# Attention on one core: when o is split, when V's remainder is taken, and where the widest exponential stands on ScalarE

## The chip, the cores and the metric

The kernel runs on one core of a Trainium2 chip. A core has TensorE (PE, matrix products; its loads of weights are PEld), VectorE (DVE), ScalarE (ACT), GpSimd (POOL) and SyncE (SP, which starts transfers). Each works through its own program in order, and they meet only at semaphores. The metric is the device time of one execution in microseconds, the median of several runs. Lower is better.

## What is computed

The reference, cut to what matters:

```python
xn = layernorm(x)                                   # x: 2 x 1024 x 256, float32
q = (xn @ Wq + bq).reshape(b, 16, t, 128)           # 16 heads, 128 columns each
k = (xn @ Wk + bk).reshape(b, t, 16, 128).transpose(0, 2, 3, 1)
v = (xn @ Wv + bv).reshape(b, t, 16, 128).transpose(0, 2, 1, 3)
weights = softmax(q @ k / sqrt(128) + causal_mask)
o = (weights @ v).transpose(0, 2, 1, 3).reshape(b, t, 2048)
result = x + (o @ Wo + bo) + ffn(xn)                # ffn: gate, up and down, weights of 4 bits
```

The change touches only the attention part.

## The kernel before

**Split products.** Every operand of a product is kept as a rounded part (`_hi`) and a remainder (`_lo`, what the rounding left out), and every product is three matmuls: hi by hi, hi by lo, lo by hi (`split_matmul`, L41 to L45). So each result in PSUM is emptied twice: ACT writes the rounded part, then DVE subtracts it from the same bank and writes the remainder. Only after both is the bank free.

**Heads and steps.** 32 heads (2 batches of 16) are worked one after the other, each in 8 steps, one for each tile of 128 query rows. Tile i needs the keys of tiles 0 to i, so its scores are (i + 1) x 128 wide; tile 7 is the widest, 1024. PE's step `i` is: the transposes of the tile three steps back (`LAG` = 3), the job that `FIRST_AT` names, the scores, the job that `EARLY_AT` names, on odd steps a product of weights with V (`with_v`), and the job that `LATE_AT` names. `with_v` in step 5 and step 7 makes quarters 0 and 1 of the head's o, in step 1 and step 3 of the next head quarters 2 and 3. Two quarters are one half of o, a full bank `O`.

**Jobs.** K0 and K1 are the two halves of the next head's K, Va and Vb parts of V, O0a to O1b products of the two halves of the last head's o with Wo. All of them use the one bank `M` (PSUM bank 5): `run` makes each wait until the one before is emptied (`job_lo_done`). Their places are K0 in step 0, K1 in 1, O0a in 2, O0b and Va in 3, O1a in 5, O1b in 6 and Vb in 7.

**A tile's way.** PE writes the scores; DVE copies them to `probs` with the mask and takes the maximum (L962); ACT takes the exponential and the row sum (`exps`, L763); POOL takes the reciprocal (L845) and scales the row (L848); three steps later PE transposes the row into one of two banks `T`, in pieces of at most 512 columns; ACT writes `pt_hi` (L749), DVE `pt_lo` (L916). A piece's transposes wait until `pt_lo` of the piece two before is written, since they reuse its bank.

**The order on ACT and DVE** is written out by hand, step by step. On ACT a step is: Va's rounding of the step before, `pt_high` of the tile three back, the `FIRST_AT` job, `o_high` (L756, in steps 0 and 4: half 0 and half 1 of the last head's o), the exponential of the tile before if that tile isn't in `EAGER`, the `EARLY_AT` job, and for tiles in `EAGER` (1, 3 and 7) their own exponential at the end. DVE has the same frame with `pt_low` (L916), `o_low` (L921), Va's remainder (L876, in step 4), the maximum (L962) and the emptying of jobs (`k_lo` L871, `acc` L883).

In heads 7, 15 and 23 the queries of the next eight heads are prepared between the steps (`q_step`, `q_ahead`, with `wq_hi` L732, `wq_lo` L889, `q_all` L904); these are called Q heads below. `q_low` and the remainders of the weights of V, K and Wo run on POOL as well.

Of the kernel before, what the change touches and what calls it, by code (L numbers as in the profile page):

```python
# [36 lines left out]
def flat(ap):  # L37
    return ap.rearrange("p a b -> p (a b)")
# [495 lines left out]
def attention(nc, sh, d, out):  # L534

    NH = BATCH * HEADS
    GROUP = N // (SEQ // HEADS)
    GROUPS = NH // GROUP
    TILES = SEQ // P
# [11 lines left out]
    with ExitStack() as c:  # L551
# [39 lines left out]
        EARLY_AT = {1: "K1", 3: "O0b", 5: "O1a"}  # L591
        LATE_AT = {3: "Va"}
        AT = [FIRST_AT[0], EARLY_AT[1], FIRST_AT[2], EARLY_AT[3], LATE_AT[3], EARLY_AT[5], FIRST_AT[6], FIRST_AT[7]]
        EAGER = (1, 3, 7)
        Q_AFTER = {2: (0,), 3: (1,), 4: (2, 3), 5: (4, 5), 6: (6, 7)}
        START = {0: ("K", 0, 1), 2: ("V", 0, 0), 4: ("V", 0, 1)}

# [22 lines left out]
        q_steps = lambda h, i: Q_AFTER.get(i, ()) if new_group(h) else ()  # L620
        eager = lambda h, i: i in EAGER or len(q_steps(h, i)) > 1

# [14 lines left out]
        def v_view(tile, pair, j):  # L637
            return tile[:, v_slots(pair), 2 * j:2 * j + 2, :]
# [55 lines left out]
        @block.scalar  # L694
        def _(act):
            def wo_high(h):
                act.wait_ge(wo_loaded, 16 * (h + 1))
                nc.scalar.activation(wo_hi[:, h % 2, :], wo_in[:], ACT.Copy).then_inc(wo_hi_done, 1)

            def vw_high(pair):  # L700
                act.wait_ge(vw_loaded, 32 * (pair + 1))
                if pair:
                    act.wait_ge(job_done, nth[("V", pair - 1, 3)])
                nc.scalar.activation(flat(vw_hi[:]), flat(vw_in[:]), ACT.Copy).then_inc(vw_hi_done, 1)

            def kw_high(pair):
                act.wait_ge(job_done, nth[("K", 2 * pair - 1, 1)])
                kv_high(nc, act, sh, 16 * (pair + 1))

            def evacuate(job):  # L710

                if job is None or job[0] == "O":
                    return
                act.wait_ge(job_done, nth[job])
                if job[0] == "K":
                    _, h, half = job
                    ins = nc.scalar.activation(k_hi[:, h % 2, half * N:(half + 1) * N], M, ACT.Identity,
                                               bias=bk[:, h % HEADS:h % HEADS + 1])
                else:
                    ins = nc.scalar.activation(v_view(v_hi, *job[1:]), M_V, ACT.Copy)  # L720
                ins.then_inc(job_hi_done, 1)

            def q_split(h, half):

                rows = q_all[:, h % GROUP, half * 32:half * 32 + 32, :].rearrange("p r c -> p (r c)")
                nc.scalar.activation(q_hi[:, half, :], rows, ACT.Copy).then_inc(q_hi_done, 1)  # L726

            def wq_high(n):

                act.wait_ge(wq_loaded[n % LOADS], 16 * (n // LOADS + 1))  # L730
                wait(act, qp_done, n - LOADS + 1)
                nc.scalar.activation(flat(wq_hi[:, n % LOADS, :, :]), flat(wq_in[:, n % LOADS, :, :]), ACT.Copy  # L732
                                     ).then_inc(wq_hi_done, 1)

            def q_ahead(o, u):

                for n in (2 * u + 2, 2 * u + 3):
                    if n < HEADS:
                        wq_high(o * HEADS + n)

            def pt_high(s):

                i = s % TILES
                for ch in range(banks_of(i)):
                    at = chunk_no(s, ch)
                    blocks = min(QT, i + 1 - ch * QT)
                    act.wait_ge(pt_done, at + 1)
                    first = pt_block(i // 2) + ch * QT
                    nc.scalar.activation(  # L749
                        pt_hi[:, first:first + blocks, i % 2 * P:(i % 2 + 1) * P],  # L750
                        T[at % 2][:, 0:blocks * P].rearrange("p (a b) -> p a b", b=P), ACT.Copy
                    ).then_inc(pt_hi_done, 1)

            def o_high(h, half):
                act.wait_ge(pv_done, 4 * h + 2 * half + 2)
                nc.scalar.activation(o_hi[:], O, ACT.Identity, bias=bv[:, h % HEADS:h % HEADS + 1]  # L756
                                     ).then_inc(o_hi_done, 1)

            def exps(s):

                act.wait_ge(max_done, s + 1)
                width = (s % TILES + 1) * P
                nc.scalar.activation(probs[:, s % 4, 0:width], probs[:, s % 4, 0:width], ACT.Exp,  # L763
                                     bias=neg_max[:, s % 16:s % 16 + 1], scale=-1.0,
                                     accum_out=row_sum[:, s % 16:s % 16 + 1]).then_inc(exp_done, 1)

            act.wait_ge(sh["bias_in"], 48)
            wq_high(0)
            wq_high(1)
            evacuate(("K", 0, 0))  # L770
            for u in range(8):
                q_ahead(0, u)
                if u == 1:
                    vw_high(0)
                evacuate(START.get(u))
            act.wait_ge(q_done, HEADS)
            q_split(0, 0)

            for s in range(NH * TILES):
                h, i = divmod(s, TILES)  # L780
                evacuate(job_of(h, LATE_AT.get(i - 1)))
                if s >= LAG:
                    pt_high(s - LAG)
                evacuate(job_of(h, FIRST_AT.get(i)))
                if i in (0, 4) and h > 0:
                    o_high(h - 1, i // 4)
                if i > 0 and not eager(h, i - 1):
                    exps(s - 1)
                evacuate(job_of(h, EARLY_AT.get(i)))
                if i == 1:  # L790
                    act.wait_ge(scores_done, s)
                    q_split(h, 1)
                    if new_group(h):
                        wq_high((h + 1) // GROUP * HEADS)
                        wq_high((h + 1) // GROUP * HEADS + 1)
                    if h % 2 == 1 and (h + 1) // 2 < NH // 2:
                        vw_high((h + 1) // 2)
                if i == 2:
                    wo_high(h)
                if i == 5 and not new_group(h) and h + 1 < NH:  # L800

                    act.wait_ge(scores_done, s)
                    q_split(h + 1, 0)
                if i == 6 and h % 2 == 0 and h // 2 + 1 < NH // 2:
                    kw_high(h // 2 + 1)
                if i == 7 and new_group(h):

                    act.wait_ge(q_done, (h + 1) // GROUP * HEADS + HEADS)
                    q_split(h + 1, 0)
                if eager(h, i):  # L810
                    exps(s)
                for u in q_steps(h, i):
                    q_ahead(h // GROUP + 1, u)

            pt_high(NH * TILES - 3)
            o_high(NH - 1, 0)
            pt_high(NH * TILES - 2)
            pt_high(NH * TILES - 1)
            o_high(NH - 1, 1)
# [42 lines left out]
        def _(dve):  # L862
# [56 lines left out]
            def o_low(h, half):  # L919
                dve.wait_ge(o_hi_done, 2 * h + half + 1)  # L920
                nc.vector.scalar_tensor_tensor(o_lo[:], O, bv[:, h % HEADS:h % HEADS + 1],  # L921
                                               o_hi[:].bitcast(F32), ALU.add, ALU.subtract).then_inc(o_lo_done, 1)
# [17 lines left out]
            for s in range(NH * TILES):  # L940
                h, i = divmod(s, TILES)
                between = FIRST_AT.get(i) == "O0a"
                if s >= LAG:
                    pt_low(s - LAG, 0)
                    if between:
                        evacuate(job_of(h, FIRST_AT[i]))
                    if banks_of((s - LAG) % TILES) > 1:
                        pt_low(s - LAG, 1)
                if not between or s < LAG:
                    evacuate(job_of(h, FIRST_AT.get(i)))  # L950
                if i in (0, 4) and h > 0:
                    o_low(h - 1, i // 4)
                if i - 1 in LATE_AT:
                    evacuate(job_of(h, LATE_AT[i - 1]))
                hurry = EARLY_AT.get(i) == "O1a"
                if hurry:
                    evacuate(job_of(h, EARLY_AT[i]))
# [6 lines left out]
                    -1.0, -MASKED, ALU.add, ALU.min, neg_max[:, s % 16:s % 16 + 1]).then_inc(max_done, 1)  # L964
                if not hurry:
                    evacuate(job_of(h, EARLY_AT.get(i)))
                if i == 1 and new_group(h):
                    wq_low((h + 1) // GROUP * HEADS)
                    wq_low((h + 1) // GROUP * HEADS + 1)
# [6 lines left out]

            end = NH * TILES
            pt_lows(end - 3)
            o_low(NH - 1, 0)
            add_residual(0)  # L980
            add_residual(1)
            evacuate(("O", NH - 1, 0, 0))
# [216 lines left out]
```

## Time and profile before

| | us |
|---|---|
| median of 3 runs | 1319.09 (1319.01 to 1320.17) |
| profiled execution, its own time | 1319.28 |
| its span | 1317.0 |

| engine | busy us | share of the span |
|---|---|---|
| PE | 1232.1 | 94% |
| PEld | 1072.9 | 81% |
| DVE | 947.8 | 72% |
| POOL | 795.8 | 60% |
| ACT | 766.3 | 58% |

The granted clock of TensorE was 0.996 of full speed over the span. The attention part runs from about 330 us to the end. A head without preparation of queries takes 26.7 us.

How to read rows of a timeline: start in us from the span's start, length in us, engine, line, operation, what is written and what is read, the shape, how many of them are merged in the row, and in brackets how long the engine sat idle before it and what released it. A row of a matmul is longer than the distance to the next one, because matmuls are pipelined.

### The profile page before, as it was taken

The page shows a single profiled execution, that of the slowest core. Times are in us where ns is not written, and L with a number is a line of the kernel's source. Part 1 is how long each engine was busy: PE and PEld are TensorE (multiplying, and loading weights), DVE is VectorE, ACT ScalarE, POOL GpSimd, SP SyncE. Part 2 cuts the span into 40 slices and gives each one's busy share as a digit, 9 for nine tenths or more (in the row PEclk, how much of TensorE's full clock was granted, in tenths as well). Part 3 has the DMA queues.
Part 4 walks back from the last instruction along what each step waited for, and adds up shares of the span by engine and source line. Part 5 has one row for each costly group of instructions (what it writes and reads, how often), then busy time and mean ns, then how long its engine had stood idle before and what let it go on. Part 6 is the DMA issues. An engine that isn't in the chain of part 4 may idle for free.

```text
span 1317.0 us, 20858 instructions
## 1 busy us (share of the span) xinstructions
PE 1232.1 (94%) x7468; PEld 1072.9 (81%) x7468; DVE 947.8 (72%) x1734; ACT 766.3 (58%) x1575; POOL 795.8 (60%) x799
## 2 busy tenths in 40 slices
PE   3799999999899999999999999999999999999997
PEld 2677777777678888888888988898888878889886
DVE  7778877888676667676766677767666776667666
ACT  3565555555446656644666665466665636566653
POOL 5566666666447667644766655366766526666662
PEclk9899999999999999999999999999999999999999
DMA  4000000010210000020000001100000110000012
GB/s 94 12 13 13 13 6 12 12 28 5 57 36 21 15 15 22 13 60 22 21 13 13 25 5 53 33 25 5 21 13 14 40 33 13 13 25 5 13 50 83
DMA packets 60986, 32.43 MB, mean 25 GB/s; under 512 B 17120, under 2 KB 60896, under 8 KB 60896
## 3 DMA queue, kind: packets, MB, share of 16 engines
q1 hardware_dynamic: 59280, 29.99, 8.1%
q10 hardware_dynamic: 1616, 1.25, 0.3%
q8 instruction: 56, 0.92, 0.3%
q14 instruction: 34, 0.28, 0.1%
HBM read 29.12 MB, written 2.10 MB: 24 GB/s over the span
## 4 chain that ended last, share of the span: by engine, by line
PE 52%; DVE 11%; ACT 8%; issue 1%; POOL 1%; DMA 0%; DVEq 0%; SPq 0%; ACTq 0%
PE ps L43 15%; PE ps L45 15%; PE ps L44 15%; PE ps L1079 7%; DVE probs L962 3%; ACT probs L763 3%; DVE pt_lo L916 2%; ACT pt_hi L749 2%; DVE o_lo L921 2%; DVE v_lo L876 1%; DVE q_all L904 1%; ACT o_hi L756 1%; ACT v_hi L720 1%; DVE wq_lo L889 1%; DVE acc L883 0%
## 5 line engine op out<-in xcount | busy, mean ns | idle before, releaser
L916 DVE TENSOR_TENSOR pt_lo<-ps,pt_hi 128x512 fp32r<-128x512 f32 (+3 forms) x384 | 204.4, 553 | 217.9 <-ACT pt_hi L749 215.1
L845 POOL TENSOR_TENSOR inv_sum<-row_sum,minus_one 128x1 f32<-128x1 f32 x256 | 141.5, 553 | 295.8 <-ACT probs L763 295.8
L848 POOL TENSOR_TENSOR probs<-probs,inv_sum 128x128 f32<-128x128 f32 (+7 forms) x256 | 296.4, 1158 | 20.1
L763 ACT ACTIVATE probs<-probs,neg_max 128x128 f32<-128x128 f32 (+7 forms) x256 | 198.5, 775 | 144.3 <-DVE neg_max L962 141.6
L749 ACT ACTIVATE pt_hi<-ps 128x512 fp32r<-128x512 f32 (+3 forms) x384 | 173.8, 488 | 93.3 <-PE ps L1079 90.4
L962 DVE CUSTOM_DVE_ANT_0 probs<-ps,mask_row 128x128 f32<-128x128 f32 (+7 forms) x256 | 192.1, 751 | 3.4 <-PE ps L45 0.7
L1079 PE MATMUL ps<-ident,probs 128*128 128x128 f32 x1152 | 172.3, 277 | 9.1 <-DVE pt_lo L916 8.4
L44 PE MATMUL ps<-pt_lo,v_hi 128*128 128x256 f32 (+1 forms) x640 | 177.5, 277 | 0.0
L45 PE MATMUL ps<-pt_hi,v_lo 128*128 128x256 f32 (+1 forms) x640 | 177.2, 277 | 0.0
L43 PE MATMUL ps<-pt_hi,v_hi 128*128 128x256 f32 (+1 forms) x640 | 170.7, 267 | 0.7 <-DVE pt_lo L916 0.7
L269 POOL TENSOR_TENSOR hid_lo<-hid,hid_hi 128x512 fp32r<-128x512 f32 x64 | 83.1, 1298 | 104.8 <-ACT hid_hi L328 104.8
L1079 PEld LDWEIGHTS ps<-ident,probs 128*128 128x128 f32 x1152 | 127.2, 140 | 20.1 <-issue 11.8
L43 PE MATMUL ps<-k_hi,q_hi 128*128 128x512 f32 (+3 forms) x384 | 140.2, 365 | 1.9 <-DVE k_lo L871 1.9
L45 PE MATMUL ps<-k_hi,q_lo 128*128 128x512 f32 (+3 forms) x384 | 133.0, 346 | 0.0
L44 PE MATMUL ps<-k_lo,q_hi 128*128 128x512 f32 (+3 forms) x384 | 132.9, 346 | 0.0
L43 PE MATMUL ps<-xn_hi,w_hi 128*128 128x512 f32 x256 | 106.2, 415 | 22.5 <-DVE hid L448 17.7
L43 PEld LDWEIGHTS ps<-pt_hi,v_hi 128*128 128x128 f32 x640 | 120.2, 188 | 6.2 <-DVE pt_lo L916 0.9
L44 PEld LDWEIGHTS ps<-pt_lo,v_hi 128*128 128x128 f32 x640 | 120.4, 188 | 5.6
L45 PEld LDWEIGHTS ps<-pt_hi,v_lo 128*128 128x128 f32 x640 | 120.6, 188 | 0.0
L825 POOL TENSOR_TENSOR q_lo<-q_all,q_hi 128x512 fp32r<-128x512 f32 x64 | 82.3, 1286 | 51.4 <-ACT q_hi L726 51.4
L45 PE MATMUL ps<-xn_hi,w_lo 128*128 128x512 f32 x256 | 103.0, 402 | 0.0
L44 PE MATMUL ps<-xn_lo,w_hi 128*128 128x512 f32 x256 | 102.8, 401 | 0.0
(109 smaller groups left out, 3006.1 us busy)
## 6 DMA issues: line engine op xcount, KB each, us to landing
wq_in<-in_wq SPq DMA_DIRECT2D x64, 128.0 KB, 2.3
kv_in<-in_wk SPq DMA_DIRECT2D x16, 256.0 KB, 2.7
kv_in<-in_wv SPq DMA_DIRECT2D x32, 128.0 KB, 2.3
wo_in<-in_wo SPq DMA_DIRECT2D x32, 128.0 KB, 2.0
q_all<-in_x SPq DMA_DIRECT2D x1, 2048.0 KB, 9.5
out<-q_all SPq DMA_DIRECT2D x8, 256.0 KB, 2.2
raw<-in_gate SPq DMA_DIRECT2D x18, 64.0 KB, 1.8
raw<-in_up SPq DMA_DIRECT2D x18, 64.0 KB, 2.0
```

What stands on the lines that cost most here:

```text
L43: nc.tensor.matmul(out, w_hi, m_hi, start=start, stop=False)
L44: nc.tensor.matmul(out, w_hi, m_lo, start=False, stop=False)
L45: return nc.tensor.matmul(out, w_lo, m_hi, start=False, stop=stop)
L269: nc.gpsimd.tensor_tensor(hid_lo[:, kk % 4, :], hid[:, kk % 4, :], hid_hi[:, kk % 4, :].bitcast(F32), ALU.subtract).then_inc(hid_lo_done, 1)
L749: nc.scalar.activation(pt_hi[:, first:first + blocks, i % 2 * P:(i % 2 + 1) * P], T[at % 2][:, 0:blocks * P].rearrange("p (a b) -> p a b", ...
L763: nc.scalar.activation(probs[:, s % 4, 0:width], probs[:, s % 4, 0:width], ACT.Exp, bias=neg_max[:, s % 16:s % 16 + 1], scale=-1.0, accum_ ...
L825: nc.gpsimd.tensor_tensor(dst, src, high.bitcast(F32), ALU.subtract).then_inc(done, 1)
L845: nc.gpsimd.tensor_tensor(inv_sum[:, at], row_sum[:, at], minus_one[:], ALU.pow).then_inc(inv_done, 1)
L848: nc.gpsimd.tensor_tensor(row, row, inv_sum[:, at].to_broadcast([P, (i + 1) * P]), ALU.mult).then_inc(probs_done, 1)
L916: nc.vector.tensor_tensor(pt_lo[where], T[at % 2][:, 0:blocks * P].rearrange("p (a b) -> p a b", b=P), pt_hi[where].bitcast(F32), ALU.subt ...
L962: nc.vector.tensor_tensor_reduce(probs[:, s % 4, 0:width], flat(S[place[("S", h, i)] % 2])[:, 0:width], mask_row[:, SEQ - width:SEQ], -1.0 ...
L1079: last = nc.tensor.transpose(T[at % 2][:, n * P:(n + 1) * P], probs[:, s % 4, b * P:(b + 1) * P], ident[:])
```

## The change

It moves instructions and removes none. On ACT and DVE, the split of half 1 of o (`o_high`, `o_low`) goes from step 4 to the end of step 3, and that of half 0 from step 0 of the next head to the end of step 7. Va's remainder on DVE goes from behind `pt_low` and `o_low` to the front of step 4. Tile 7 is no longer in `EAGER`: its exponential goes from the end of step 7 to step 0 of the next head, behind `pt_high` of tile 5 and K0's rounding. The last head's has a place of its own behind the loop. PE's, POOL's and SP's programs are the same.

```diff
-        EAGER = (1, 3, 7)
+        EAGER = (1, 3)
...
                 evacuate(job_of(h, FIRST_AT.get(i)))
-                if i in (0, 4) and h > 0:
-                    o_high(h - 1, i // 4)
-                if i > 0 and not eager(h, i - 1):
+                if i > 0 and not eager(h, i - 1) or i == 0 and h > 0:
                     exps(s - 1)
...
                 if eager(h, i):
                     exps(s)
+                if i == 3 and h > 0:
+                    o_high(h - 1, 1)
+                if i == 7:
+                    o_high(h, 0)
                 for u in q_steps(h, i):
                     q_ahead(h // GROUP + 1, u)
 
+            exps(NH * TILES - 1)
             pt_high(NH * TILES - 3)
-            o_high(NH - 1, 0)
             pt_high(NH * TILES - 2)
...
                 between = FIRST_AT.get(i) == "O0a"
+                if i - 1 in LATE_AT:
+                    evacuate(job_of(h, LATE_AT[i - 1]))
                 if s >= LAG:
                     pt_low(s - LAG, 0)
...
-                if i in (0, 4) and h > 0:
-                    o_low(h - 1, i // 4)
-                if i - 1 in LATE_AT:
-                    evacuate(job_of(h, LATE_AT[i - 1]))
...
                 if not hurry:
                     evacuate(job_of(h, EARLY_AT.get(i)))
+                if i == 3 and h > 0:
+                    o_low(h - 1, 1)
+                if i == 7:
+                    o_low(h, 0)
...
             pt_lows(end - 3)
-            o_low(NH - 1, 0)
             add_residual(0)
```

DVE at the turn from step 3 to step 4 of one head (`acc` is O0b's, `v_lo` Va's, `pt_lo` of tile 1, the maximum of tile 4), before:

```order
327 L883 TENSOR_TENSOR acc<-ps,acc 128x512
328 L916 TENSOR_TENSOR pt_lo<-ps,pt_hi 128x2x128
329 L921 SCALAR_TENSOR_TENSOR o_lo<-ps,bv,o_hi 128x512
330 L876 TENSOR_TENSOR v_lo<-ps,v_hi 128x2x256
331 L962 ISA probs,neg_max<-ps,mask_row 128x640
```

and after:

```order
327 L885 TENSOR_TENSOR acc<-ps,acc 128x512
328 L923 SCALAR_TENSOR_TENSOR o_lo<-ps,bv,o_hi 128x512
329 L878 TENSOR_TENSOR v_lo<-ps,v_hi 128x2x256
330 L918 TENSOR_TENSOR pt_lo<-ps,pt_hi 128x2x128
331 L962 ISA probs,neg_max<-ps,mask_row 128x640
```

The lines of the code are two later there. `pt_lo` went behind both; `o_lo` is ahead of `v_lo` still, but in step 3.

ACT from the exponential of tile 6 to K1's rounding, across the end of a head (`pt_hi` of 4 and 2 blocks is tile 5, of 4 and 3 tile 6; the two `k_hi` are K0 and K1), before:

```order
321 L763 ACTIVATE probs,row_sum<-probs,neg_max 128x896
322 L763 ACTIVATE probs,row_sum<-probs,neg_max 128x1024
323 L749 ACTIVATE pt_hi<-ps 128x4x128
324 L749 ACTIVATE pt_hi<-ps 128x2x128
325 L717 ACTIVATE k_hi<-ps,bk 128x512
326 L756 ACTIVATE o_hi<-ps,bv 128x512
```

and after:

```order
321 L763 ACTIVATE probs,row_sum<-probs,neg_max 128x896
322 L756 ACTIVATE o_hi<-ps,bv 128x512
323 L749 ACTIVATE pt_hi<-ps 128x4x128
324 L749 ACTIVATE pt_hi<-ps 128x2x128
325 L717 ACTIVATE k_hi<-ps,bk 128x512
326 L763 ACTIVATE probs,row_sum<-probs,neg_max 128x1024
```

The exponential of tile 7 and `o_hi` changed places; the three instructions between them stand as before. On DVE, `o_lo` went with it, from behind `k_lo` of K0 to ahead of `pt_lo` of tile 5:

```order
306 L962 ISA probs,neg_max<-ps,mask_row 128x1024
307 L962 ISA neg_max 128x1
308 L923 SCALAR_TENSOR_TENSOR o_lo<-ps,bv,o_hi 128x512
309 L918 TENSOR_TENSOR pt_lo<-ps,pt_hi 128x4x128
310 L918 TENSOR_TENSOR pt_lo<-ps,pt_hi 128x2x128
311 L873 SCALAR_TENSOR_TENSOR k_lo<-ps,bk,k_hi 128x512
```

This is DVE after; before, `o_lo` stood behind the last of these rows.

## Rows read from the trace of the kernel before

**Rows 1.** Busy time, 700 to 800 us: length, PE, PEld, DVE, ACT, POOL, clock, DMA.
```profile
700.00:800.00 100.00, 97.83 (x673) 89.02 (x673) 68.16 (x142) 64.41 (x140) 66.74 (x75) 1.00 0.05 14
```

**Rows 2.** List of waits of PE, 330 to 1300 us: who, for whom, us, times, longest.
```profile
PE ps L43 <- DVE v_lo L876: 8.6, 27, 0.3
PE ps L1079 <- DVE pt_lo L916: 8.4, 31, 1.6
```

**Rows 3.** Timeline, head 12, steps 5 and 6, PE; columns: start us, length us, instruction.
```profile
731.57 0.28 PE L45 MATMUL ps<-k_hi,q_lo 128*128 128x256 f32 x1
732.17 0.50 PE L43 MATMUL ps<-o_hi,wo_hi 128*128 128x512 f32 x1 [0.32 <-DVE v_lo L876]
...
733.98 0.50 PE L43 MATMUL ps<-o_hi,wo_hi 128*128 128x512 f32 x1
```

**Rows 4.** Timeline, step 4 of the same head (12), ACT.
```profile
729.28 0.60 ACT L720 ACTIVATE v_hi<-ps 128x512 fp32r<-128x512 f32 x1 [2.70 <-PE ps L45]
...
730.04 0.69 ACT L756 ACTIVATE o_hi<-ps,bv 128x512 fp32r<-128x512 f32 x1
```

**Rows 5.** Timeline, steps 4 and 5, DVE.
```profile
730.77 0.75 DVE L921 SCALAR_TENSOR_TENSOR o_lo<-ps,bv,o_hi 128x512 fp32r<-128x512 f32 x1 [0.15 <-ACT o_hi L756]
731.43 0.68 DVE L876 TENSOR_TENSOR v_lo<-ps,v_hi 128x512 fp32r<-128x512 f32 x1
732.03 0.81 DVE L962 CUSTOM_DVE_ANT_0 probs<-ps,mask_row 128x640 f32<-128x640 f32 x1
...
733.24 0.68 DVE L883 TENSOR_TENSOR acc<-ps,acc 128x512 f32<-128x512 f32 x1
```

**Rows 6.** Timeline, step 0 to step 2 of head 12, PE.
```profile
713.99 0.84 PE L1079 MATMUL ps<-ident,probs 128*128 128x128 f32 x6
...
716.71 0.95 PE L1079 MATMUL ps<-ident,probs 128*128 128x128 f32 x7 [0.21 <-DVE pt_lo L916]
...
717.74 0.28 PE L45 MATMUL ps<-k_hi,q_lo 128*128 128x256 f32 x1
717.85 0.43 PE L43 MATMUL ps<-xn_hi,kv_hi 128*128 128x512 f32 x1
...
721.27 1.06 PE L1079 MATMUL ps<-ident,probs 128*128 128x128 f32 x8
```

**Rows 7.** Timeline, the same place, ACT.
```profile
714.11 1.15 ACT L763 ACTIVATE probs<-probs,neg_max 128x1024 f32<-128x1024 f32 x1 [1.04 <-DVE neg_max L962]
...
715.26 0.85 ACT L749 ACTIVATE pt_hi<-ps 128x512 fp32r<-128x512 f32 x2
716.26 0.69 ACT L717 ACTIVATE k_hi<-ps,bk 128x512 fp32r<-128x512 f32 x1
```

**Rows 8.** Timeline, the same place, DVE.
```profile
715.87 1.02 DVE L916 TENSOR_TENSOR pt_lo<-ps,pt_hi 128x512 fp32r<-128x512 f32 x2 [1.79 <-ACT pt_hi L749]
716.98 0.75 DVE L871 SCALAR_TENSOR_TENSOR k_lo<-ps,bk,k_hi 128x512 fp32r<-128x512 f32 x1
```

**Rows 9.** Timeline, the same place, POOL, and one scaling of 640 columns.
```profile
715.43 0.55 POOL L845 TENSOR_TENSOR inv_sum<-row_sum,minus_one 128x1 f32<-128x1 f32 x1
716.06 1.90 POOL L848 TENSOR_TENSOR probs<-probs,inv_sum 128x1024 f32<-128x1024 f32 x1
...
734.52 1.25 POOL L848 TENSOR_TENSOR probs<-probs,inv_sum 128x640 f32<-128x640 f32 x1
```

**Rows 10.** Timeline, step 4 of head 15, DVE, POOL and PE.
```profile
816.27 0.75 DVE L921 SCALAR_TENSOR_TENSOR o_lo<-ps,bv,o_hi 128x512 fp32r<-128x512 f32 x1
...
819.64 0.76 DVE L889 TENSOR_TENSOR wq_lo<-wq_in,wq_hi 128x256 fp32r<-128x256 f32 x2 [1.29 <-ACT wq_hi L732]
...
820.01 1.51 POOL L848 TENSOR_TENSOR probs<-probs,inv_sum 128x640 f32<-128x640 f32 x1
...
820.22 0.47 PE L43 MATMUL ps<-xn_hi,wq_hi 128*128 128x512 f32 x1 [0.99 <-DVE wq_lo L889]
```

**Rows 11.** Timeline, behind the last head, PE.
```profile
1296.87 0.47 PE L43 MATMUL ps<-o_hi,wo_hi 128*128 128x512 f32 x1 [2.01 <-DVE o_lo L921]
```
## The prediction, made before the result

> **What bounds the kernel now.** I read the busy times of a stretch first, then the list of waits, then the timelines of one head, engine by engine. In a stretch of 100 us in the middle of the attention part TensorE (PE) is busy for 97.8 us, while VectorE (DVE) has 68, ScalarE (ACT) 64 and GpSimd (POOL) 67 [rows 1]. PE issues the same work before and after the change, so the time falls only by what PE stops waiting. The list of waits is therefore what matters, and in it the lines of PE alone [rows 2]: 27 waits for v_lo of 0.32 us each, and 31 for pt_lo, of which 30 are 0.2 us and one is 1.6 us. The far longer waits of POOL, DVE and ACT cost nothing as long as PE does not stand behind them.
>
> An idle time of PE in these rows is smaller than the loss. A matmul's row lasts 0.28 us but the next starts 0.11 us after it (717.74 and 717.85 in [rows 6]), so 0.17 us of drain is counted as busy. A v_lo wait costs 0.32 + 0.17 = 0.49 us of start to start, a pt_lo wait 0.21 + 0.17 = 0.38 us.
>
> **Place one: V's remainder, step 4.** In step 5 PE wants to start O1a, the product of o with Wo, into the bank M. M must be free of V's rows, that is v_lo of job Va must be written. O1a starts at 732.17 where the matmul in front started at 731.57: without the wait it would start at 731.68 [rows 3]. v_hi is written by 729.88 [rows 4], but DVE first takes pt_lo of tile 1, then waits for o_hi and does o_lo, and only then v_lo at 731.43 for 0.68 us, up to 732.11 [rows 5]. PE starts 0.06 us later. Now o_hi and o_lo stand at the end of step 3. Their input is complete before Va is issued, so they fall into time in which ACT sat idle for 2.70 us [rows 4]: 0.69 us on ACT and 0.75 us on DVE at no cost. The new wait of ACT for the product holds nothing up, since what is queued behind it is v_hi, which cannot start before 729.28. On DVE v_lo is next, at 729.9, done at 730.6, over 1 us before PE wants it. pt_lo of tile 1 moves behind it, to 730.5; its reader is PE's product of quarter 0, behind O1a. The maximum of tile 4 starts at about 730.9 and not 732.03, so that ScalarE's exponential and POOL's scaling behind it run earlier too.
> What is late next after O1a: O1b needs M back from DVE's addition of O1a. That addition was held by DVE until 733.24 and now starts when O1a ends, at 732.7, done at 733.4. O1b would start 0.49 us earlier than its 733.98 [rows 3, 5], at 733.49. It fits with less than 0.1 us to spare. I take the whole 0.49 us: 27 x 0.49 = 13.2 us. The lower bound is 27 x 0.32 = 8.6 us, if only the visible idle time goes; nothing excludes less if O1b takes the wait over, which I price among the rivals.
>
> **Place two: the end of a head.** In step 1 PE's transposes of tile 6 start at 716.71, behind a wait for pt_lo of tile 5, whose bank they reuse [rows 6]. ACT did the exponential of tile 7 (1024 wide, 1.15 us from 714.11) ahead of pt_hi of tile 5 at 715.26 [rows 7], though the transposes of that tile had started at 713.99. DVE's pt_lo then came at 715.87 [rows 8]. Now ACT does o_hi first. It waits for the product of quarter 1, the last thing that PE issues before 713.99; with the drain of 0.17 us that is 714.2, and o_hi ends at 714.9. pt_hi of tile 5 then starts at 714.8. DVE does o_lo at 714.9 and starts pt_lo of tile 5 0.66 us later (the spacing of o_lo and v_lo in [rows 5]), at 715.57: 0.30 us earlier. The transposes of tile 6 could start at 716.4, where they would start without any wait at 716.33. So this wait nearly goes.
> But **another stands behind it**. K0 and K1, the two halves of the next head's K, share the bank M. K0's k_hi starts when PE ends K0, at 716.26, and k_lo follows from 716.98 to 717.73 [rows 7, 8]. Neither moves: K0 is issued ahead of the wait, and both engines are free by then, ACT 0.85 us after 714.8. K1 started at 717.85 [rows 6], 0.12 us behind k_lo. 0.38 us earlier would be 717.47, before k_lo is done. With the 0.06 us that PE needed behind v_lo it starts at 717.79. So the head gains 0.06 us, and 0.3 us of PE's wait moves from the transposes to K1. 30 x 0.06 = 1.8 us, with bounds of 0 (if PE needs 0.12 us behind k_lo) and 30 x 0.38 = 11.4 us (if k_lo does not hold K1). I take 1.8, since both of its ends are rows of this place. The last head has no K0 and K1, and its wait of 1.6 us shrinks by the 0.30 us of pt_lo.
> The Trainium skill (Perfetto Trace Analysis, section Matmuls) says that independent groups of matmuls should rotate through different PSUM banks, so that emptying one overlaps the next group. M doesn't rotate here. By that rule a bubble at K1 is to be expected as soon as nothing earlier hides it; no row of before shows one there. By the rule the sum is as above, by the missing row it would be 9.6 us more.
>
> **The exponential that is now late.** It starts behind k_hi of K0, at 716.26 + 0.59 = 716.85 and not 714.11. ACT went on 1.15 us after its start [rows 7], so 718.0, and I allow 0.15 us until POOL has the row sum: 718.15. POOL's scaling starts 0.63 us behind its reciprocal and takes 1.90 us [rows 9]: done at 720.7, against 717.96 before. PE wants it for the transposes of tile 7 at 721.27 - 0.06 = 721.21 [rows 6]. The cover is 0.5 us, so it costs nothing; without it each 0.1 us would cost 3.1 us over 31 heads. pt_hi and pt_lo of tile 6 also come behind the exponential, at 718.0 and 718.7; their reader is the same place of PE, at 721.2. On POOL the scaling of tile 0 and q_lo are queued behind the scaling of tile 7; they are wanted in step 3 and step 4.
> Against this speaks a rule of the Trainium skill (SBUF — State Buffer, section Who interferes with whom): a VectorE tensor_tensor with both inputs in SBUF contends with GpSimd's reads, and the pair of ports is held for a whole instruction. In a head that prepares Q, wq_lo is such an instruction and comes in the step after. The trace agrees that there is a price, but a small one: a 640 wide scaling beside wq_lo took 1.51 us against 1.25 us without [rows 9, 10]. A hold for both of the wq_lo would be 0.76 us [rows 10]. By the row the cover holds, by the rule 0.25 us would be lost in each of 3 heads, 0.8 us in all.
>
> **Q heads, and the tail.** In heads 7, 15 and 23 PE does not wait for v_lo but in step 4 for wq_lo: 0.99 us at 820.22 [rows 10]. The chain is o_lo (816.27), v_lo, maximum of tile 4, its exponential, wq_hi, wq_lo. o_lo leaves it, and with it its 0.66 us: 3 x 0.65 = 1.9 us. Bounds: 0, if wq_in arrives late, and that. At the very end PE waits 2.01 us for o_lo of the last head [rows 11]. o_lo is early now, but the last exponential comes ahead of pt_hi still and o_hi ahead of both, so DVE reaches the two additions of the residual and then O0a's at the same time as before, and O0b waits for that. I count 0, between -0.2 and +1.3.
>
> **The sum.** 13.2 + 1.8 + 0.3 + 1.9 + 0 = 17.2 us. The profiled execution took 1319.28 us (1317.0 span and 2.3 around it), which gives 1302.1; the median before is 0.2 lower. I say **1302.0**.
>
> **The rivals.**
> (a) k_lo does not hold K1, because the step between is longer than I read. For it: no wait there now. Against: it is 0.12 us of slack and 0.38 us are taken. It gives 9.6 us more, 1292.4.
> (b) Half of place one comes back in the same head: O1b then waits for the addition of O1a, or Vb for that of O1b. For it: under 0.1 us of slack. Against: the addition moves with PE. 27 x 0.25 = 6.7 us less, 1308.7.
> (c) Slower: the scaling of tile 7. If POOL ends it after 721.21, PE stands at tile 7's transposes in all 31 heads. For it: 2.7 us later with 3.3 us of room. Against: 0.5 us are left. From 0.55 + 0.52 = 1.1 us more delay the kernel is slower than before. A delay of 1.5 us would lose 31 x 1.0 = 30 us against a gain of 17, 1331.
> (d) The waits that the list names are not what holds PE, and the same time stands elsewhere: 1319.
>
> **How the numbers follow.** Forecast, 1299 to 1305.5: 0.67. (a) 0.08, (b) 0.14 (1305.5 to 1312), (c) 0.07, (d) 0.04. The range is 1296 to 1309.5: it takes in the forecast, the near half of (b), and the group heads and the tail at either bound; (a) and (c) stay outside. Faster by over 0.2% (2.6 us, about what a measurement can tell from no change) 0.89, within 0.04, slower 0.07.
>
> **What would show it.** Right: no waits of PE for v_lo in the list, the 30 pt_lo waits at most 0.1 us, and in their place some 30 waits of PE for k_lo of 0.1 to 0.2 us idle; heads that repeat 0.55 us faster; a wq_lo wait near 0.35 us in step 4. Wrong: waits of PE for POOL's probs at tile 7, or for acc at O1b, or 27 waits for v_lo that are only shorter.

## The result, and the profile after

The changed kernel took 1300.53 us (median of 4 runs, 1299.12 to 1301.17), the kernel before on the same chip 1319.55 us (4 runs, 1319.01 to 1320.17). The ratio is 0.9854, with a 95% interval of 0.9837 to 0.9871. The predicted time was 1302.0, 1.5 us above the measured one. The profiled execution took 1301.17 us, 18.1 less than the 1319.28 of before; the sum had said 17.2.

Busy time from 700 to 800 us of the changed kernel, with the columns of [rows 1]:

```profile
700.00:800.00 100.00, 99.73 (x680) 90.67 (x680) 72.92 (x149) 66.68 (x149) 68.65 (x76) 1.00 0.05 16
```

TensorE went from 97.8 to 99.7. The lines of its list of waits from 330 to 1300 us that matter here (who, for whom, us in total, times, longest), which answer [rows 2]:

```profile
PE ps L43 <- DVE wq_lo L891: 3.0, 6, 0.7
PE ps L43 <- DVE k_lo L873: 1.9, 1, 1.9
PE ps L1082 <- DVE pt_lo L918: 1.9, 2, 1.3
PE ps L43 <- DVE o_lo L923: 1.7, 1, 1.7
```

The 27 waits for v_lo are gone. Of the 31 for pt_lo one is left, that of the last head (1.3 us, before 1.6); the other of these two, 0.6 us, is new and stands in the tail. Only 1.9 us are put down to k_lo, all of it one wait in head 0 that was there before too. The o_lo line is no new wait either: it is at the last half of o, and before the change it fell behind 1300 us. The 30 short waits for k_lo that the prediction put there don't stand in this list.

**Place one.** DVE from step 3 on, then PE at O1a, which answer [rows 5] and [rows 3]:

```profile
722.08 0.75 DVE L923 SCALAR_TENSOR_TENSOR o_lo<-ps,bv,o_hi 128x512 fp32r<-128x512 f32 x1 [2.19 <-ACT o_hi L756]
723.46 0.69 DVE L878 TENSOR_TENSOR v_lo<-ps,v_hi 128x512 fp32r<-128x512 f32 x1 [0.63 <-ACT v_hi L720]
...
726.13 0.69 DVE L885 TENSOR_TENSOR acc<-ps,acc 128x512 f32<-128x512 f32 x1 [0.44 <-PE ps L45]
```

```profile
725.11 0.28 PE L45 MATMUL ps<-k_hi,q_lo 128*128 128x256 f32 x1
725.23 0.39 PE L43 MATMUL ps<-o_hi,wo_hi 128*128 128x512 f32 x1
725.46 0.39 PE L44 MATMUL ps<-o_lo,wo_hi 128*128 128x512 f32 x1
...
726.94 0.48 PE L43 MATMUL ps<-o_hi,wo_hi 128*128 128x512 f32 x1
```

v_lo ends at 724.15, 1.08 us before O1a. O1a starts 0.12 us after the start of the matmul in front, where it had been 0.60. DVE's addition of O1a now waits for PE, not the other way round, and ends at 726.82; O1b starts 0.12 us behind it, where it was due by PE's own order.

**Place two.** PE at the end of a head and behind it, DVE and POOL at the same place, which answer [rows 6, 8, 9]:

```profile
708.13 0.47 PE L43 MATMUL ps<-xn_hi,kv_hi 128*128 128x512 f32 x1
...
709.95 0.96 PE L1082 MATMUL ps<-ident,probs 128*128 128x128 f32 x7
710.99 0.28 PE L45 MATMUL ps<-k_hi,q_lo 128*128 128x256 f32 x1
711.33 0.50 PE L43 MATMUL ps<-xn_hi,kv_hi 128*128 128x512 f32 x1
711.66 0.39 PE L44 MATMUL ps<-xn_lo,kv_hi 128*128 128x512 f32 x1
714.82 1.06 PE L1082 MATMUL ps<-ident,probs 128*128 128x128 f32 x8
```

```profile
709.13 1.01 DVE L918 TENSOR_TENSOR pt_lo<-ps,pt_hi 128x512 fp32r<-128x512 f32 x2
710.52 0.75 DVE L873 SCALAR_TENSOR_TENSOR k_lo<-ps,bk,k_hi 128x512 fp32r<-128x512 f32 x1 [0.39 <-ACT k_hi L717]
```

```profile
712.33 1.90 POOL L850 TENSOR_TENSOR probs<-probs,inv_sum 128x1024 f32<-128x1024 f32 x1
```

The first row is K0. The transposes of tile 6 no longer stand behind pt_lo in the list: they start 1.82 us behind K0, where it was 2.12 (K0 at 714.59, the transposes at 716.71 in [rows 6]). K1 starts at 711.33, 0.06 us behind the end of k_lo (711.27) and 0.34 us after the start of the matmul in front: the wait that the prediction named is there. POOL ends the scaling of tile 7 at 714.23, 0.59 us before PE transposes it at 714.82. Where PE does stand on this scaling (exp_late and pool_long below) it starts 0.06 us behind it, so 0.53 us of that distance is cover. The forecast, counted in the same way, was 0.5.

**Where the wait for k_lo shows.** TensorE's weight loads have a list of waits of their own (same columns, 330 to 1300 us). Of before:

```profile
PEld ps L43 <- DVE v_lo L876: 14.2, 27, 0.5
...
PEld ps L43 <- DVE k_lo L871: 0.7, 1, 0.7
```

and of after:

```profile
PEld ps L43 <- DVE k_lo L873: 8.7, 31, 0.5
```

Here are the v_lo waits that went and the k_lo waits that came: 30 of 0.27 us at K1, and one of 0.5 us in head 0 that was there before (the 0.7 above). In PE's list the 30 are missing because a wait of 0.22 us start to start leaves only some 0.06 us of idle time behind the drain of the matmul in front (711.27 to 711.33), too little for a row of its own. Drain means here the part of a matmul's row that lasts beyond the due start of the next one, 0.17 us for 0.28 - 0.11. These lists also say **which instruction a wait holds: the weight load**, and through it the matmul. (In the program `run` issues the wait ahead of the job's first matmul, whose load comes first.) The loads around O1a, before the change:

```profile
731.45 0.19 PEld L45 LDWEIGHTS ps<-k_hi,q_lo 128*128 128x128 f32 x1
732.17 0.19 PEld L43 LDWEIGHTS ps<-o_hi,wo_hi 128*128 128x128 f32 x1 [0.53 <-DVE v_lo L876]
```

and after:

```profile
725.00 0.19 PEld L45 LDWEIGHTS ps<-k_hi,q_lo 128*128 128x128 f32 x1
725.12 0.19 PEld L43 LDWEIGHTS ps<-o_hi,wo_hi 128*128 128x128 f32 x1
```

Without a wait the load runs 0.11 us ahead of its matmul (725.12 and 725.23), under the matmul in front. With one, load and matmul are both recorded at 732.17, and the matmul's row is longer: the next one starts at 732.50, 0.33 us later, where without a wait it is 0.23 (725.46). So each such wait costs 0.10 us more than the distance between the starts shows.

**The whole sum again.** From K0 of one head to K0 of the next took 26.71 us before (714.59 to 741.28 and the like) and 26.11 after (708.13 to 734.23). The chain from K0 of head 1 to K0 of head 30 went from 848.98 to 831.86 us, 17.1 less: 26 plain heads at 0.59 and 1.7 in the three Q heads. Behind it 1.1 us went (0.6 in head 30, 0.3 in the last head, 0.2 in the tail). Ahead of it 0.1 us was lost, the rest of two larger amounts: step 0 of head 0 came 1.2 us sooner, and head 0 then took 1.35 us longer, since the granted clock of TensorE was 0.59 and 0.56 of full speed in the 4 us from 378 us on (between its levels of 1.2 and 2.4 GHz), behind an idle time of PE of 1.9 us; in the kernel before it stayed at 1.00 behind the same idle time. Six of the twelve profiled executions have such a dip there (one_only has it, o_early does not), so it is not put down to the change.

### The profile page after: what moved, and what is told of

It reads as the page before. It is cut to its first block, busy times and chain, and to the rows that moved or that the text cites. A ratio compares the mean times of both kernels' runs of the same rounds, so it can differ in the third digit from the quotient of the medians.

```text
span 1299.0 us, 20858 instructions
## 1 busy us (share of the span) xinstructions
PE 1229.7 (95%) x7468; PEld 1072.4 (83%) x7468; DVE 952.5 (73%) x1734; ACT 766.3 (59%) x1575; POOL 795.5 (61%) x799
## 4 chain that ended last, share of the span: by engine, by line
PE 64%; DVE 5%; ACT 3%; issue 1%; POOL 1%; DMA 0%; DVEq 0%; SPq 0%; ACTq 0%
PE ps L43 19%; PE ps L45 19%; PE ps L44 19%; PE ps L1082 8%; DVE k_lo L873 2%; ACT k_hi L717 2%; DVE q_all L906 1%; DVE wq_lo L891 1%; DVE pt_lo L918 0%; DMA wq_in<-in_wq 0%; DVE acc L885 0%; ACT probs L763 0%; POOL probs L850 0%; ACT wq_hi L732 0%; DVE probs L962 0%
## 5 line engine op out<-in xcount | busy, mean ns | idle before, releaser
L923 DVE SCALAR_TENSOR_TENSOR o_lo<-ps,bv,o_hi 128x512 fp32r<-128x512 f32 x64 | 48.1, 751 | 96.1 <-ACT o_hi L756 96.1
```

## The experiments

The ratios are to the kernel before on the same chip, with their 95% intervals:

| kernel | median us | ratio to before | one head, us |
|---|---|---|---|
| kernel before | 1319.6 | 1 | 26.71 |
| changed kernel | 1300.5 | 0.9854 (0.9837 to 0.9871) | 26.11 |
| one_only | 1302.6 | 0.9866 (0.985 to 0.9883) | 26.10 |
| two_only | 1319.8 | 0.9998 (0.9988 to 1.0008) | 26.70 |
| v_first | 1308.0 | 0.9915 (0.9899 to 0.9932) | 26.21 |
| o_early | 1301.6 | 0.9866 (0.985 to 0.9883) | 26.10 |
| exp_late | 1322.7 | 1.0018 (1.0008 to 1.0027) | 26.76 |
| pool_128 | 1300.7 | 0.9857 (0.9842 to 0.9872) | 26.10 |
| pool_long | 1316.2 | 0.9973 (0.9964 to 0.9982) | 26.63 |
| k1_split | 1290.5 | 0.9781 (0.9768 to 0.9794) | 25.79 |
| one_split | 1323.0 | 1.0024 (1.0015 to 1.0034) | 26.84 |
| split_exp_eager | 1325.5 | 1.0045 (1.0029 to 1.0062) | 26.85 |

My theory was that of the prediction: place one brings nearly all, place two is held by k_lo at bank M, the late exponential stays under its cover. Rivals: place two is worth more than it seems; the cover is larger or smaller than the rows say; what stands at K1 is not bank M.

### Each place alone

**one_only**, against before (`o_high` goes to the end of ACT's step 3, `o_low` on DVE moves the same way, and `evacuate` of Va's remainder stands at the front of DVE's step):

```diff
-                if i in (0, 4) and h > 0:
-                    o_high(h - 1, i // 4)
+                if i == 0 and h > 0:
+                    o_high(h - 1, 0)
+                if i == 3 and h > 0:
+                    o_high(h - 1, 1)
...
+                if i - 1 in LATE_AT:
+                    evacuate(job_of(h, LATE_AT[i - 1]))
```

> The kernel before with place one alone: half 1 of o is split at the end of step 3 and V's remainder comes first in step 4; half 0 of o and the exponential of tile 7 stay where they were. Theory A (the gain is the v_lo wait in front of O1a and the shorter chain in the Q heads; place two only trades a wait of the transposes for one of K1): 17 to 18 us faster than before, 1301.5, no waits of PE for v_lo, the 31 waits for pt_lo unchanged, K1 not waiting for k_lo. Rival B (place two gives a good part of the gain, as the 0.38 us of its wait would suggest): 1308 or slower.

**two_only**, against before (DVE has the same moves of `o_low`):

```diff
-        EAGER = (1, 3, 7)
+        EAGER = (1, 3)
...
-                if i in (0, 4) and h > 0:
-                    o_high(h - 1, i // 4)
+                if i == 4 and h > 0:
+                    o_high(h - 1, 1)
-                if i > 0 and not eager(h, i - 1):
+                if i > 0 and not eager(h, i - 1) or i == 0 and h > 0:
...
+                if i == 7:
+                    o_high(h, 0)
```

> The kernel before with place two alone: half 0 of o at the end of step 7, the exponential of tile 7 behind K0's rounding; half 1 of o and V's remainder as before. Theory A: within 1 us of before, 1319, with 27 waits for v_lo as before, the pt_lo waits at the end of the heads gone, and K1 starting 0.06 us behind the end of k_lo. Rival B: 30 x 0.3 us faster, 1310.

one_only brings 17 of the 19 us, two_only none that can be measured; each is as Theory A said. The intervals are some 2 us wide on either side, so they don't tell one_only from the changed kernel. PE and DVE of two_only behind the end of a head:

```profile
744.77 0.28 PE L45 MATMUL ps<-k_hi,q_lo 128*128 128x256 f32 x1
745.12 0.50 PE L43 MATMUL ps<-xn_hi,kv_hi 128*128 128x512 f32 x1
```

```profile
744.32 0.75 DVE L873 SCALAR_TENSOR_TENSOR k_lo<-ps,bk,k_hi 128x512 fp32r<-128x512 f32 x1 [0.39 <-ACT k_hi L717]
```

k_lo ends at 745.07 and K1 starts at 745.12. In its lists the pt_lo waits are gone and the loads of K1 wait 30 times for k_lo (8.8 us with the one wait of head 0): the wait has moved and the time has not.

### The two halves of place one

**v_first** takes V's remainder to the front of DVE's step and leaves o where it was:

```diff
+                if i - 1 in LATE_AT:
+                    evacuate(job_of(h, LATE_AT[i - 1]))
                 if s >= LAG:
...
                     o_low(h - 1, i // 4)
-                if i - 1 in LATE_AT:
-                    evacuate(job_of(h, LATE_AT[i - 1]))
```

> The kernel before with V's remainder first in step 4 and nothing else; o is still split in step 4, now behind it. Theory A says that either order alone frees O1a: v_lo done 1 us before it is wanted, o_lo done at 731.6 where O1a wants it at 731.68, so 26 to 27 x 0.6 = 16 us faster, 1303.5, nothing in the Q heads since o_lo is still ahead of the maximum there. Rival C: o_lo then takes the place of v_lo as what O1a waits for, and less than half is gained, over 1311.

**o_early** is one_only without that move: half 1 of o goes to the end of step 3, V's remainder stays behind `pt_low`.

```diff
-                if i in (0, 4) and h > 0:
-                    o_high(h - 1, i // 4)
+                if i == 0 and h > 0:
+                    o_high(h - 1, 0)
+                if i == 3 and h > 0:
+                    o_high(h - 1, 1)
```

> The kernel before with half 1 of o split at the end of step 3 and nothing else; V's remainder still stands behind pt_lo of tile 1. Theory A: v_lo ends at about 731.2, 0.5 us before O1a wants it, so the whole gain of place one, the Q heads' 1.7 us too: 17.5 us faster, 1302. Rival C: V's place is what counts, and here under half of it is gained, over 1311.

o_early gave the same as one_only. So at place one the early split of o is the whole gain, and V's remainder first adds nothing to it. v_first reached about two thirds, 4.5 us less than I expected and 5.4 less than one_only. The only waits for o_lo in PE's list of v_first are the two behind the last head, yet there is one at each O1a. PE, and DVE:

```profile
727.48 0.28 PE L45 MATMUL ps<-k_hi,q_lo 128*128 128x256 f32 x1
727.65 0.47 PE L43 MATMUL ps<-o_hi,wo_hi 128*128 128x512 f32 x1
727.96 0.39 PE L44 MATMUL ps<-o_lo,wo_hi 128*128 128x512 f32 x1
```

```profile
726.77 0.74 DVE L921 SCALAR_TENSOR_TENSOR o_lo<-ps,bv,o_hi 128x512 fp32r<-128x512 f32 x1
```

O1a starts 0.14 us behind the end of o_lo (727.51), 0.17 us after the start of the matmul in front and 0.31 us ahead of the next. Against the changed kernel's 0.12 and 0.23 that is 0.13 us, and the head took 0.10 to 0.12 more, 3.2 us or less in 27 heads. The rest is the Q heads: there o_lo is still in the chain to wq_lo, and PE waited 5.0 us for wq_lo in all, against 3.0 in one_only.

### The late exponential and its cover

**exp_late** moves only the exponential of tile 7, against before. o keeps its old places:

```diff
-        EAGER = (1, 3, 7)
+        EAGER = (1, 3)
...
-                if i > 0 and not eager(h, i - 1):
+                if i > 0 and not eager(h, i - 1) or i == 0 and h > 0:
```

> The kernel before with one edit: the exponential of tile 7 goes to step 0 of the next head, behind K0's rounding and behind o_hi, which stays there. Theory A: the transposes of tile 6 stop waiting, K1 waits for k_lo instead, and the exponential is 0.6 us later than in the changed kernel, so that POOL ends the scaling of tile 7 0 to 0.2 us behind the time at which PE wants it: 0 to 6 us slower than before, 1319 to 1325, with waits of PE for POOL's probs. Rival E: the late exponential costs nothing, 1317 to 1319.

**pool_128** and **pool_long** leave the result as it is and put idle work on POOL ahead of tile 7's reciprocal, in the changed kernel: one multiplication of 128 columns (some 0.4 us), and three of 120 columns (1.07 us). pool_long:

```diff
+                if i == 7:
+                    for u in range(3):
+                        part = extra[:, u * 120:(u + 1) * 120]
+                        nc.gpsimd.tensor_tensor(part, part, minus_one[:].to_broadcast([P, 120]), ALU.mult)
```

pool_128 has `extra[:]` with `to_broadcast([P, 128])` in the place of `part`, once:

```diff
+                if i == 7:
+                    nc.gpsimd.tensor_tensor(extra[:], extra[:], minus_one[:].to_broadcast([P, 128]), ALU.mult)
```

> The changed kernel with one multiplication of 128 columns more on POOL in the same place, about 0.4 us, less than the cover of 0.55 us. Theory A: 1300.5, no change, at most 0.1 us in each head, 1303. If PE already stood at the scaling of tile 7: 31 x 0.4 us slower, 1313.

> The changed kernel with three multiplications of 120 columns more on POOL, into a tile that nobody reads, between the exponential of tile 7 and its reciprocal; some 1.1 us later scaling of tile 7. Theory A: the cover is 0.55 us, so about 0.5 us are lost in each of 31 heads: 1316, and PE waits for probs at tile 7. If the cover were the whole 3 us that the scaling had before: 1300.5.

In pool_128 the scaling starts 4.54 us behind K0 and not 4.19, 0.35 us later, and the cover swallows that whole: the head stays at 26.10. In pool_long PE stands at the transposes of tile 7; its list of waits, and POOL and PE of one head:

```profile
PE ps L1089 <- POOL probs L857: 10.9, 32, 0.7
```

```profile
717.53 1.07 POOL L853 TENSOR_TENSOR extra<-extra,minus_one 128x120 f32<-128x120 f32 x3 [2.68 <-ACT probs L764]
...
719.19 1.89 POOL L857 TENSOR_TENSOR probs<-probs,inv_sum 128x1024 f32<-128x1024 f32 x1
```

```profile
720.55 0.27 PE L45 MATMUL ps<-pt_hi,v_lo 128*128 128x128 f32 x1
721.14 0.55 PE L1089 MATMUL ps<-ident,probs 128*128 128x128 f32 x3 [0.32 <-POOL probs L857]
```

PE starts 0.06 us behind the scaling (721.08). The scaling starts 5.23 us behind K0, 1.04 us later than in the changed kernel (the three extra rows overlap a little, so it is less than their 1.07). Beyond the cover that is 1.04 - 0.53 = 0.51 us; the head took 0.52 us longer, 15.6 us in 30 heads, and 15.5 us were lost against pool_128. (30 of the 32 waits in the list are these; the other two are in head 0 and in the last head.) So rival (c)'s mechanism is real, and its price is what exceeds the cover, in every head. By these numbers the changed kernel would be slower than before from 0.53 + 18.1 / 31 = 1.1 us of delay, as the prediction had it; that is an estimate, no run stands at that point. In exp_late nothing is saved to pay for the move, and the scaling starts 4.77 us behind K0, 0.58 us later than in the changed kernel. There o_hi still stands between K0's rounding and the exponential, so the scaling (1.89 us from 720.23) ends at 722.12, and PE takes tile 7 at 722.18. These short waits stand in no list, but PE starts 0.05 to 0.06 us behind the scaling in every head. It cost 2 to 3 us, inside what was expected, and 0.05 us a head is 1.5 of them. That o_hi left that place is what gives the changed kernel its cover.

### Is it bank M that holds K1?

**k1_split** is the changed kernel with the first 3 of the 18 matmuls of quarter 2 of o, which have no need of bank M, moved from behind K1 to ahead of it:

```diff
-            def with_v(h, q):
+            def with_v(h, q, part=slice(0, 8)):
...
-                for s in range(2 * q + 2):
+                for s in range(2 * q + 2)[part]:
...
-                last.then_inc(pv_done, 1)
+                if part.stop == 8:
+                    last.then_inc(pv_done, 1)
...
+                ahead = 1 if i == 1 and h > 0 else 0
+                if ahead:
+                    with_v(h - 1, 2, slice(0, ahead))
...
-                    with_v(ph, pi // 2)
+                    with_v(ph, pi // 2, slice(ahead, 8))
```

> The changed kernel, and in step 1 PE issues the first 3 of the 18 matmuls of quarter 2 ahead of K1 instead of behind it: 0.34 us of work into the place where K1 waits for k_lo. Theory A (K1 stands behind k_lo for 0.23 us of start to start, and its first matmul is slower by 0.06 us behind a wait): 30 x 0.25 to 0.3 us faster than the changed kernel, 1292 to 1293, no K1 start right behind k_lo. Rival D: the 0.23 us is the matmuls' own distance and not a wait, 1300.5, or the scaling of tile 7 comes due and takes half of it back, 1296.

PE of k1_split, behind the scores of step 1:

```profile
706.83 0.28 PE L45 MATMUL ps<-k_hi,q_lo 128*128 128x256 f32 x1
706.95 0.28 PE L43 MATMUL ps<-pt_hi,v_hi 128*128 128x256 f32 x1
707.07 0.28 PE L44 MATMUL ps<-pt_lo,v_hi 128*128 128x256 f32 x1
707.18 0.28 PE L45 MATMUL ps<-pt_hi,v_lo 128*128 128x256 f32 x1
707.31 0.40 PE L43 MATMUL ps<-xn_hi,kv_hi 128*128 128x512 f32 x1
707.54 0.39 PE L44 MATMUL ps<-xn_lo,kv_hi 128*128 128x512 f32 x1
```

The three matmuls take 0.36 us (706.95 to 707.31), k_lo ends at 707.12, and K1's load and first matmul follow without a gap. The head is 0.32 us shorter: 0.22 us of start (0.34 where 0.12 is due) and 0.10 us of the first matmul (0.33 where 0.23 is due). Over the 30 heads that have both K1 and an early quarter 2 that is 9.6 us, and 10.0 lie between the medians. I had expected 7.5 to 9 us, 1292 to 1293: the exposed load was priced at 0.06 us and is 0.10. **This is the best version of the study**: 1290.54 us (1289.2 to 1291.3), faster than both kernels. It leaves less cover: the scaling of tile 7 now ends 0.29 us before PE transposes it, where it was 0.59.

It is also what rival (a) promised, 1292.4, by another way. The Trainium skill (Perfetto Trace Analysis, section Matmuls) wants independent groups of matmuls in different banks, so that emptying one overlaps the next group. The trace bears the bubble out, 0.32 us a head. Here work for another bank in between removed it; no run has a second bank for the jobs, so the two ways were not compared.

### What place two is worth then

**one_split** has the same three matmuls early, on one_only instead of the changed kernel. Against one_only (`with_v` as above):

```diff
+                ahead = 1 if i == 1 and h > 0 else 0
+                if ahead:
+                    with_v(h - 1, 2, slice(0, ahead))
...
-                    with_v(ph, pi // 2)
+                    with_v(ph, pi // 2, slice(ahead, 8))
```

> Place one alone (one_only) with the early 3 matmuls of quarter 2 ahead of K1. There o_lo of half 0 is still in step 0, done 0.5 us after K1 wants to start, and the early matmuls write into the bank that it reads. Theory A: PE waits for o_lo ahead of K1, 0.9 us in each head, the wait of tile 6 unchanged: 20 to 28 us slower than one_only, 1322 to 1330. Rival F (the three early matmuls bring their gain without place two): 1293.

**split_exp_eager** is k1_split with the exponential of tile 7 back at the end of step 7, ahead of o's half 0:

```diff
-        EAGER = (1, 3)
+        EAGER = (1, 3, 7)
...
-                if i > 0 and not eager(h, i - 1) or i == 0 and h > 0:
+                if i > 0 and not eager(h, i - 1):
```

> k1_split with one edit taken back: the exponential of tile 7 is done at the end of step 7 again, ahead of o_hi of half 0 and of pt_hi of tile 5. It asks what the late exponential is worth once K1 no longer waits. Theory A: pt_lo of tile 5 comes behind the exponential, o_hi and o_lo, some 0.9 us of wait at the transposes of tile 6 in each head, so 25 to 30 us slower than k1_split, 1316 to 1320. Rival F (with K1 split, the place of the exponential is of no account): 1291.

one_split is 20 us slower than one_only, inside the expected 20 to 28. Its list of waits of PE, and one of those places:

```profile
PE ps L43 <- DVE o_lo L923: 15.0, 30, 0.5
PE ps L1083 <- DVE pt_lo L918: 8.4, 31, 1.6
```

```profile
720.39 0.36 PE L43 MATMUL ps<-pt_hi,v_hi 128*128 128x256 f32 x1 [0.50 <-DVE o_lo L923]
```

Both halves of o use the one bank `O`. Quarter 2 begins half 1, and the bank is free only when o_lo of half 0 is done, at its old place behind k_lo; it ends at 720.24 and PE starts at 720.39. In split_exp_eager o is early, but ACT takes the exponential first, then o_hi, then pt_hi of tile 5:

```profile
715.20 1.15 ACT L763 ACTIVATE probs<-probs,neg_max 128x1024 f32<-128x1024 f32 x1 [1.05 <-DVE neg_max L961]
...
716.35 0.67 ACT L756 ACTIVATE o_hi<-ps,bv 128x512 fp32r<-128x512 f32 x1
716.92 0.85 ACT L749 ACTIVATE pt_hi<-ps 128x512 fp32r<-128x512 f32 x2
```

```profile
718.55 0.96 PE L1081 MATMUL ps<-ident,probs 128*128 128x128 f32 x7 [0.98 <-DVE pt_lo L917]
```

The wait for pt_lo grows from the 0.21 us of before to 0.98: the transposes of tile 6 start 2.89 us behind K0, where it is 1.82 in k1_split, and the head takes 1.05 us longer. split_exp_eager is 35.0 us slower than k1_split: 30.2 us from K0 of head 1 to K0 of head 30, and 5.0 behind it, 1.0 each in head 30 and the last head and the rest in the tail. The sign was as expected, the loss 5 to 10 us larger; the expected 0.9 us a head was short by 0.15, and the tail was not in the sum. The moves of place two, then, gain nothing that can be measured by themselves, and k1_split needs them: without both it is 32 us slower (one_split), without the late exponential 35.

## Why the prediction was right, point by point

- **What bounds the kernel.** PE's waits were the right list: PE issues the same work, and the time fell by what it stopped waiting.
- **Place one: right, and its term 2.7 us too small.** All 27 waits went, O1a's start came 0.48 us nearer as said, and rival (b) did not happen: O1b starts 1.71 us behind O1a where it was 1.81, so it came forward by all of it, and it starts 0.38 us behind PE's transposes of that step, as before. The step that was short is "0.32 + 0.17 = 0.49 us of start to start". It leaves out the weight load, which stood in the wait as well and made the first matmul 0.10 us longer. 27 x 0.59 = 15.9, not 13.2. o_early shows that the early split of half 1 of o is all of it.
- **Place two: the mechanism right, the 0.06 us not gained.** k_lo holds K1, and the 0.34 us between two matmul starts there is what k1_split takes away. That K1 "started at 717.85, 0.12 us behind k_lo" was a reading of the wrong engine: k_lo had held K1's weight load already before. The loads, and the matmul behind K1's first, before the change:

```profile
717.62 0.19 PEld L45 LDWEIGHTS ps<-k_hi,q_lo 128*128 128x128 f32 x1
717.78 0.19 PEld L43 LDWEIGHTS ps<-xn_hi,kv_hi 128*128 128x128 f32 x1
```

```profile
718.12 0.40 PE L44 MATMUL ps<-xn_lo,kv_hi 128*128 128x512 f32 x1
```

  K1's load starts 0.05 us behind k_lo (717.73), 0.16 us after the load in front where 0.12 is usual, and 3.19 us behind K0 (714.59); in the changed kernel it is 0.06 behind k_lo and 3.20 behind K0 (711.33 and 708.13). The matmul's start did come the forecast 0.06 us nearer to K0, 3.20 where it was 3.26, but its distance to the next one grew by as much, from 0.27 (717.85 to 718.12) to 0.33 (711.33 to 711.66): the second matmul stands 3.53 us behind K0 in both kernels. There was no slack to take, 0 and not 1.8 us. two_only measured 0.9998.
- **Rival (a)** fell by the same rows, and by two_only; rival (d) fell with the time and the list.
- **The late exponential: right.** Cover 0.53 us, forecast 0.5. pool_128 and pool_long give both sides of it. The rule in the Trainium skill (SBUF — State Buffer, section Who interferes with whom), which would have cost 0.8 us in the Q heads, had no occasion to: the prediction put wq_lo beside the scaling of tile 7, but in the changed kernel that scaling has ended before the first wq_lo of each Q head starts (by 4.4, 0.35 and 0.35 us), and it takes its usual 1.9 us there. So the forecast of no loss held, and the rule was not tested by it. Elsewhere the trace of before has a row for such a hold, off TensorE's path: one wq_lo at 562.86 took 1.30 us beside POOL's q_lo (562.60 to 563.88), where it otherwise takes 0.42.
- **Q heads: right, 1.7 us of 1.9.** PE's wait for wq_lo at the place of [rows 10] is now:

```profile
811.41 0.47 PE L43 MATMUL ps<-xn_hi,wq_hi 128*128 128x512 f32 x1 [0.36 <-DVE wq_lo L891]
```

  0.36 us, forecast 0.35. Two of the three heads gained 0.65; the third gained 0.42. There wq_hi stood behind the arrival of wq_in (2.5 us of idle time on ACT, in the other two 0.9), and PE waited 1.04 us for q_all, where it was 0.87 before.
- **Last head and tail**: 0.3 and 0.2 us, forecast 0.3 and 0. The wait of 2.0 us for o_lo in [rows 11] is gone, and 0.6 us for pt_lo and 0.6 us for acc, at O0b, stand in its place.
- **What would show it** held for v_lo, pt_lo, wq_lo and the heads (0.60 us each, forecast 0.55). It failed for the 30 waits for k_lo "in the list": they are in the list of the weight loads.

The two errors of size (+2.7 and -1.8 us) nearly cancel, so that the sum came out within 0.9 us of the profiled 18.1 is in part luck; both come from the same omission, the weight load. The measured medians lie 19.0 us apart with an interval of about 2 us on either side.

## What to carry to other kernels

Read the weight loads' waits and starts beside the matmuls': where the program waits ahead of a load, the wait costs the drain and the exposed load on top of the idle time shown, and one that is little longer than the drain (here 0.22 us against 0.17) is not in the matmuls' list at all. Where a bank is handed from a job to the next with both its emptyings between them, put a few matmuls that need another bank in the gap, and first take out of that other bank what still occupies it. A long instruction can go behind short ones that others wait for as long as its own reader's distance is known; that distance, less the time the reader needs behind it, is the budget, and what exceeds it was paid in full in every head.

## What the runs showed of the hardware

- **A wait of TensorE costs more than its idle time**: the idle time, 0.17 us of drain of the matmul in front (one of 256 columns), and 0.10 us in which the first matmul is longer since its weight load has no matmul to hide under (0.33 us to the next start, 0.23 without a wait).
- **From the end of what TensorE waits for to its start** it took 0.05 to 0.06 us behind v_lo and k_lo, 0.05 to 0.06 behind POOL's scaling (pool_long, exp_late), and 0.11 to 0.15 us behind o_lo (its load in v_first, its matmul in one_split). Why o_lo is slower I didn't settle.
- **Handing one bank on** (K0's start to K1's first load) takes 3.20 us here, the two emptyings of 0.69 and 0.75 us included. It was 3.19 before and 3.21 in k1_split (703.98 to 707.19).
